# Two heads of each four get their band from VectorE in float32, two from TensorE in three bf16 parts

## The reference, cut to what matters

```python
def _L1_attn_ref(x, Wq, Wk, Wv, Wo, rel, ln_gamma, ln_beta):      # 16 heads, DH = 16, T = 1024
    xn = _layernorm(x, ln_gamma, ln_beta)
    q = proj(Wq) / math.sqrt(DH); k = proj(Wk); v = proj(Wv)
    scores = jnp.einsum('bhid,bhjd->bhij', q, k)
    dist = jnp.clip(i[:, None] - i[None, :], 0, MAX_REL)           # MAX_REL = 128
    scores = scores + rel[:, dist][None]                           # a bias for each head and distance
    scores = jnp.where(causal[None, None], scores, -jnp.inf)
    attn = jax.nn.softmax(scores, axis=-1)
    y = jnp.einsum('bhij,bhjd->bhid', attn, v)
    return x0 + y @ Wo.T
```

## Time and profile before

| | |
|---|---|
| median of 3 runs | 2776.13 us (2773.8 to 2779.16) |
| profiled execution | 2777.85 us, its span 2776.0 us, mean granted clock 0.863 |
| TensorE busy | 2217.6 us (80%), weight loads 1613.4 us |
| VectorE busy | 1620.4 us (58%) |
| ScalarE, GpSimd busy | 969.2 us (35%), 453.9 us (16%) |
| heads stage, from the first score to the last | 1843.9 to 2580.8 us |

### The profile page before, as it was taken

One profiled execution on the slowest core, in us unless ns is written; L12 is line 12 of the kernel. 1 busy time (PEld: TensorE's weight loads), 2 busy tenths in 40 slices (PEclk: granted clock), 3 DMA queues, 4 the chain that ended last, 5 costly groups with the idle time before them and its releaser, 6 DMA issues.

```text
span 2776.0 us, 39998 instructions
## 1 busy us (share of the span) xinstructions
PE 2217.6 (80%) x13342; PEld 1613.4 (58%) x13342; DVE 1620.4 (58%) x4577; ACT 969.2 (35%) x1964; POOL 453.9 (16%) x402
## 2 busy tenths in 40 slices
PE   4489999908999857999994276378999999999476
PEld 2478888806888736888883144324444454444254
DVE  6744443353555675433444897266866766875695
ACT  4122233203333331232331331325555556556321
POOL 4320000040000134000003553411011011000242
PEclk8799999958999878999997555669999999999755
DMA  7110101020000122001002100242322323230001
GB/s 237 41 59 26 28 28 32 22 76 1 1 1 1 35 83 73 28 28 32 28 28 60 49 12 0 61 65 59 48 42 53 48 47 63 37 43 2 5 22 39
DMA packets 83735, 114.14 MB, mean 41 GB/s; under 512 B 12162, under 2 KB 74020, under 8 KB 80420
## 3 DMA queue, kind: packets, MB, share of 16 engines
q1 hardware_dynamic: 77396, 94.53, 15.5%
q0 software_dynamic: 6144, 17.05, 1.9%
HBM read 68.90 MB, written 42.64 MB: 40 GB/s over the span
## 4 chain that ended last, share of the span: by engine, by line
PE 63%; DVE 21%; ACT 5%; issue 5%; DMA 3%; POOL 2%; another core or an unknown queue 1%; SPq 0%; ACTq 0%; DVEq 0%; POOLq 0%
PE psum L774 9%; PE psum L776 9%; PE psum L775 9%; PE psum L122 5%; PE psum L2097 4%; PE psum L123 4%; PE psum L124 4%; PE psum L2076 4%; PE psum L2056 3%; PE psum L861 3%; PE psum L2080 3%; DVE junk L1961 2%; PE psum L1426 2%; DVE m L1949 1%; DVE stats L155 1%
## 5 line engine op out<-in xcount | busy, mean ns | idle before, releaser
L1898 ACT ACTIVATE pt<-psum 128x512 f32<-128x512 f32 (+3 forms) x768 | 338.9, 491 | 283.2 <-DVE psum L1987 196.2
L739 DVE SCALAR_TENSOR_TENSOR h<-psum,xg,sg 128x128 f32<-128x128 f32 x592 | 166.9, 345 | 415.2 <-PE psum L861 415.2
L774 PE MATMUL psum<-w_hi,xt_hi 128*128 (+1 forms) x720 | 286.3, 398 | 33.7 <-DVE xt_lo L704 33.7
L548 ACT ACTIVATE sg<-psum 128x512 f32<-128x512 f32 x180 | 107.6, 598 | 584.0 <-PE psum L776 543.0
L775 PE MATMUL psum<-w_lo,xt_hi 128*128 (+1 forms) x720 | 284.5, 395 | 0.0
L776 PE MATMUL psum<-w_hi,xt_lo 128*128 (+1 forms) x720 | 284.5, 395 | 0.0
L2056 PE MATMUL psum<-ks,qs 96*128 96x512 bf16 (+3 forms) x768 | 232.9, 342 | 49.7 <-DMA ks<-qk_scr 19.9
L2076 PE MATMUL psum<-qs,ks 99*128 99x512 bf16 (+3 forms) x768 | 236.8, 332 | 18.4 <-ACT pt L1898 11.4
L774 PE MATMUL psum<-w_hi,ht_hi 128*128 (+1 forms) x720 | 220.5, 306 | 8.3 <-DVE x L754 8.0
L1961 DVE CUSTOM_DVE_ANT_0 junk<-psum,band_q 128x256 bf16<-128x256 f32 (+1 forms) x512 | 204.8, 400 | 22.3 <-PE psum L2056 12.0
L776 PE MATMUL psum<-w_hi,ht_lo 128*128 (+1 forms) x720 | 205.9, 286 | 0.0
(11 more groups left out here) (281 smaller groups left out, 4884.4 us busy)
## 6 DMA issues: line engine op xcount, KB each, us to landing
xg<-w_dram SPq DMA_DIRECT2D x54, 256.0 KB, 3.3
qk_scr<-parts SPq DMA_DIRECT2D x32, 384.0 KB, 2.5
qs<-qk_scr SPq DMA_DIRECT2D x96, 128.0 KB, 7.0
ks<-qk_scr SPq DMA_DIRECT2D x96, 128.0 KB, 7.7
xg<-rows_in SPq DMA_DIRECT2D x74, 132.0 KB, 2.2
rows_out<-yb SPq DMA_DIRECT2D x74, 128.0 KB, 1.7
x<-x_dram SPq DMA_DIRECT2D x4, 1024.0 KB, 9.3
out_dram<-x SPq DMA_DIRECT2D x4, 1024.0 KB, 4.4
```

Source lines behind the costliest of these rows:

```text
L739: ins = dve.scalar_tensor_tensor(out=h[i % 2][:, e, :], in0=u[:, e, :], scalar=xg[j % XSLOT][:, at:at + 1], in1=sg[i % 2][:, e, :], op0=AL ...
L774: pe.matmul(out, a[0], b[0], start=first, stop=False)
L1898: act.activation(pt[n % NPT][:, 0:q1 - q0], st_bank(n)[:, 0:q1 - q0], ACT.Exp).then_inc(*exped.up())
```

## The change: what it does

`HP` becomes 2 in the heads and their tables. Heads 0 and 1 of each four keep the three-part addition on TensorE; heads 2 and 3 are added by VectorE from a `band_dve` with room for two heads. `HEAD_OF` changes from (3, 0, 1, 2) to (3, 0, 2, 1), so the positions alternate: VectorE, TensorE, VectorE, TensorE. In the tables a pair of heads goes one way or the other (`by_pe`): pairs for TensorE are split into three parts, pairs for VectorE are copied once in float32 and have one step fewer in the list. Comments and renumbered waits aside:

```diff
+        HP = 2
-                self.band_dve = sb(stack, "band_dve", [P, NHG, 2 * P])
+                self.band_dve = sb(stack, "band_dve", [P, NHG, HG - HP, 2 * P])
+                self.dve_ok = S("band_dve")
@@ order of the tables
-                    yield [("part", (hp, 2))]
+                    if self.by_pe(hp):
+                        yield [("part", (hp, 2))]
+            def by_pe(self, hp):
+                return 2 * hp % HG < HP
+            def parts_of(self, hp, part):
+                return 3 * (hp // 2) + part + 1
@@ tables, GpSimd
-                elif kind == "part" and i[1] < 2:
+                elif kind == "part" and i[1] < 2 and self.by_pe(i[0]):
@@ tables, ScalarE
                     act.wait_ge(*self.flipped(i + 1))
+                    if i and not self.by_pe(i - 1):
+                        act.wait_ge(*self.dve_ok((i + 1) // 2))
...
-                        if n < 2:
-                            act.activation(self.band_dve[:, g, :], self.full[:, n, :], ACT.Copy)
+                        if not self.by_pe(hp):
+                            act.activation(self.band_dve[:, g, :, :], self.full[:, :, :],
+                                           ACT.Copy).then_inc(*self.dve_ok.up())
@@ heads
-        HEAD_OF = (HG - 1, *range(HG - 1))
+        HEAD_OF = (HG - 1, 0, HG - 2, 1)
@@ heads, ScalarE
-                                act.wait_ge(*biased(u * len(near_cells) + near_cells.index(cell) + 1))
+                                act.wait_ge(*biased((u * len(near_cells) + near_cells.index(cell)) * (HG - HP) + (HEAD_OF[pos] < HG - 1) + 1))
@@ heads, VectorE
-                                dve.tensor_tensor(at, at, band_dve[:, i[0] % NHG, q0 - j * P:b1 - j * P],
+                                dve.tensor_tensor(at, at, band_dve[:, i[0] % NHG, h - HP, q0 - j * P:b1 - j * P],
```

More of the change, by code:

```diff
@@ L1482, in staged @@
                 return S.dma(f"stage_in{m % 2}")(m // 2 + 1)
+            def by_pe(self, hp):
+                return 2 * hp % HG < HP
             def heads_of(self, hp):
                 g, h0 = divmod(2 * hp, HG)
-                return g, h0, min(2, HP - h0)
+                return g, h0, 2
+            def parts_of(self, hp, part):
+                return 3 * (hp // 2) + part + 1
             def on_sp(self, kind, i):
@@ L1544, in on_pool @@
                     now = (self.full, self.left)[part]
-                    pool.wait_ge(*self.part_ok(3 * hp + part + 1))
+                    pool.wait_ge(*self.part_ok(self.parts_of(hp, part)))
                     pool.tensor_tensor(self.left[:, 0:n, :], now[:, 0:n, :], self.band[:, part, g, h0:h0 + n, :],
@@ L1562, in on_act @@
                         act.wait_ge(*self.fulled(hp + 1))
-                        if n < 2:
-                            act.activation(self.band_dve[:, g, :], self.full[:, n, :], ACT.Copy)
-                    else:
-                        act.wait_ge(*self.left_ok(2 * hp + part))
-                    act.activation(self.band[:, part, g, h0:h0 + n, :], now[:, 0:n, :],
-                                   ACT.Copy).then_inc(*self.part_ok.up())
+                        if not self.by_pe(hp):
+                            act.activation(self.band_dve[:, g, :, :], self.full[:, :, :],
+                                           ACT.Copy).then_inc(*self.dve_ok.up())
+                    elif self.by_pe(hp):
+                        act.wait_ge(*self.left_ok(2 * (hp // 2) + part))
+                    if self.by_pe(hp):
+                        act.activation(self.band[:, part, g, h0:h0 + n, :], now[:, 0:n, :],
+                                       ACT.Copy).then_inc(*self.part_ok.up())
                     if part == 1:
```

## The result

The changed kernel takes 2784.13 us (median of 7 runs, 2782.27 to 2787.86); the kernel before, run beside it on the same chip, 2774.61 us (7 runs). The ratio is 1.0038, 95% interval 1.0027 to 1.0048: slower by 0.38%, or 9.5 us. The prediction was 2779 us: the time is 0.2% above it and lies in its range of 2760 to 2796. The change itself was forecast at +2.7 us, less than the 5.5 us that it took for measurable, and came out more than three times as large. "Slower" had a chance of 0.32, "the same" 0.43.

A forecast was written before the change was run, and what follows sets the result against it. TensorE looked full in a plain group (36.77 of 37.80 us), VectorE equally full in its last five cells (12.93 of 13.90). Terms +7.6, +0.3, -3.5 and -1.7 gave +2.7 us on 2776.13, so 2779 us, range 2760 to 2796.

The forecast's parts named there:

- TensorE's saving doesn't arrive: Plain groups: the fourth score waits for the first score's exponential, so at most 1.0 of 2.5 us saved can arrive.
- the last group: Final group of scores, without maxima beside it: fourth score waits for the exponential, so no gain was taken.
- VectorE in the last five cells: End of a group: VectorE's additions make TensorE end 0.54 us later, bounds 0 and 1.12; 14 groups, +7.6 us.
- plain groups: Seven groups without a projection beside them: 38.2 to 38.6 us each; about +0.04 us in their first seven cells.
- Groups with a projection: Seven groups beside a projection or output product: 0.5 us gain each in their first part, -3.5 us together.
- So this is hidden: Cell of a plain group: third exponential, ending near 2210.0, delays nothing; its bank is needed after 2210.40.
- a band taken out ahead of such a wait is lost: First part of groups with a projection: TensorE waits at the projection's chain; gain bounds 0 and 1.5 us, 0.5 taken.
- the last piece is the same: Last five cells of groups with a projection: 13.90 us with VectorE busy 12.93, as in plain groups, so +0.54 us.
- Tables: Stage before the heads: less GpSimd work gives back VectorE time, -1.7 us, bounds 0 and -4.
- The middle case: Whole kernel: saving and additions cancel, +2.7 us; own range 2770.6 to 2781.6 us, chance 0.43.
- TensorE's time comes free: Scores: the saving arrives, up to 39.9 us (2736), half of it about 2758 us; chance 0.25, 0.05 for the whole.
- VectorE becomes the bound: Scores: additions in the last five cells pass on in full, 1.12 us in 14 groups; +20 us, 2796; chance 0.32.

The follow-up runs named there:

- e1_order: Changed kernel with the heads of each cell in the order TensorE, VectorE, TensorE, VectorE (0, 3, 1, 2); 0.9983 of the kernel before.
- e8_after_lead: Changed kernel with the maxima 1.2 instead of 1.5 groups ahead of the scores; 0.9967 of the kernel before.
- e4_both: Changed kernel in which TensorE also makes three band matmuls for head 2, beside VectorE's addition; 1.0044 of the kernel before.
- e5_old_tables: Changed kernel with the old splitting work in the tables, its results put into a spare tile; 1.0050 of the kernel before.
- e6_after_again: Changed kernel run again unchanged, on the chip of the old-tables run; 1.0033 of the kernel before.
- e3_none: Changed kernel without VectorE's addition for head 2 and ScalarE's wait for it, so head 2 gets no band; 0.9988 of the kernel before.
- e7_order_lead: Changed kernel with head order 0, 3, 1, 2 and the maxima 1.2 instead of 1.5 groups ahead; 0.9908 of the kernel before.
- e11_order_lead_11: Changed kernel with head order 0, 3, 1, 2 and the maxima 1.1 instead of 1.5 groups ahead; 0.9983 of the kernel before.
- e10_before_order_lead: Kernel before with head order 0, 3, 1, 2 and the maxima 1.2 instead of 1.5 groups ahead; 0.9995 of the unedited kernel before.
- e9_before_lead: Kernel before with only the maxima moved to 1.2 instead of 1.5 groups ahead; 0.9984 of the unedited kernel before.

## Why the prediction was right where it was, and where not

**TensorE's saving doesn't arrive: right.** Of 2.5 us a group, 0.28 us (without the additions) or 0.14 us (with them) arrive; "at most 1.0 us" was the bound; the value taken was 0.15 us, in the cell of the earlier trace rows. e1_order shows that the wait on the first head's exponential is the reason in the last group and a part of it in the others. I had taken nothing for the last group; it was -0.33 us.

**VectorE in the last five cells: right, a little over.** Forecast +0.54 us and VectorE 13.9 busy of 14.4; measured +0.50 and 13.76 of 14.40. The plain groups' 38.2 to 38.6 us came as 38.33. e8_after_lead shows the cause by taking it away. Both hold in e4_both, so it is the additions and not the lighter TensorE.

**Groups with a projection: wrong.** The term was -0.5 + 0.54 for each group and measured +1.1. The step that failed is "In the cell of the earlier trace rows the third exponential would end near 2210.0; the score that needs its bank is the second of the next cell ... So this is hidden", carried over from a plain group's cell to all groups. In groups 4 and 8 VectorE's order holds the normalisation ahead of the late addition, and the next cell's second score waits: +0.35 and +0.52 us in that cell, +0.74 and +0.93 in the early cells together. With it failed "a band taken out ahead of such a wait is lost ... I take 0.5" of gain: the early cells where the clock is alike gave +0.9 us over the seven groups, not -3.5. That "the last piece is the same" was read in group 5; it holds there and in groups 9 and 12, but in group 4 the last five cells take 17.70 us, not 13.90. Their term was near all the same: +2.9 against 7 x 0.54 = 3.8. The room that I read for VectorE (43.96 of 66.21 us) was again a mean over a stretch, the very error that I had avoided for the plain group by cutting it into pieces. The other half of the growth, 4.0 us, lies in cells that also have another length at half clock, for which the sum had no term. That the late addition holds the next cell is shown; how those 4.0 us divide between the change and the clock is open.

**Tables: right in kind, too small.** -1.7 us forecast, -2.7 (e5_old_tables against e6_after_again) to -3.6 measured, inside the bounds 0 and -4.

**Luck.** That 2779 us is within 0.2% of the measured time says little, since the whole forecast change was 0.1% of it. The kernel before also came out 1.5 us lower beside the changed one than in the three runs that the prediction used, and the tables gave back 1.9 us of the miss. The middle case's own range, 2770.6 to 2781.6, does not hold 2784.13.

**The rivals.** "TensorE's time comes free" is excluded for this kernel by e3_none, and became true in part in e7_order_lead (1.4 of 2.5 us in a plain group, 37.70 to 36.28), by the two conditions that the prediction gave for it: a fourth score that isn't held, and last cells that take their additions into VectorE's gaps. "VectorE becomes the bound" is right for the last five cells, at half of its price of 1.12 us. The whole came out between it and the forecast. The Trainium skill's rule on the most-contended engine ("Perfetto Trace Analysis", "Identifying the Most-Contended Engine") would have had VectorE, busy 81% of a plain group, as the engine to spare; read so, the change is a loss, and the sign agrees. But e7_order_lead has VectorE busy 33.30 of 36.28 us and gains by the same change: the share alone does not decide, the place does.

## What to carry to other kernels

Moving work between engines that wait for each other through a few banks pays only if three places are looked at: the wait that holds the engine you relieve, the stretch in which the engine you load is already full, and what else stands in that engine's order ahead of the new instruction, in each kind of stretch and not just the commonest. A change that loses by itself may be the better half of one that wins: here one line of order and one number turned +0.4% into -0.9%, and neither helped the kernel before by more than 0.2%. When one engine's load is uneven, shift its light stretch to where the new work falls before you give the change up.

## What the runs showed of the hardware that I had not expected

TensorE's time at half clock within the scores part varied from 29.6 to 50.9 us (e7_order_lead, e11_order_lead_11) between kernels with the same instructions in another order, and from 17.4 to 34.8 (e10_before_order_lead, e9_before_lead) between variants of the kernel before. In e11_order_lead_11 it reached a plain group (13, 38.78 us with 3.4 at half clock) and the last group. The same kernel's group 4 took 68.28 and 69.92 us in two executions. With so much of it, by my estimate, differences under some 0.2% between two such kernels say little of their logic. The kernel before took 2748.4, 2748.9 and 2773.7 us on three chips, and 2774.6 in the first measurement, whose chip is not on record: up to 0.9% apart, as much as the best gain found here.
